# LoRA up projection in split precision instead of float32 in an attention plus mixture-of-LoRA kernel

## The reference

```
x = x + layernorm(attention(layernorm(x), wq, wk, wv, wo))       # 32 heads of 16, 8 kv heads, rotary, causal
n = layernorm(x)
h = n @ A^T            (8 experts x rank 16 = 128 columns)
logits = n @ W_gate^T  (8 experts), the two largest get softmax weights, the others 0
hw = h * (weight of its expert)
x = x + layernorm(n @ W_base^T + b_base + hw @ B)                # hw @ B: 128 -> 512, the LoRA up product
```

## Time and profile before

| | us |
|---|---|
| three runs | 270.4, 269.82, 265.75 |
| median of the runs | 269.82 |
| span of the profiled execution, first to last instruction | 265.6 |
| busy in it: PE, DVE, ACT, POOL | 212.1, 170.5, 135.9, 117.9 |

### The profile page before, as it was taken

How to read it: one execution, slowest core, us unless ns; L and a number is a source line. 1 busy time by engine, 2 the same in 40 slices (tenths; PEclk the granted TensorE clock), 3 DMA queues, 4 the chain that set the end, 5 groups by cost and what they waited for, 6 DMA issues and landing times.

```text
span 265.6 us, 3792 instructions
## 1 busy us (share of the span) xinstructions
PE 212.1 (80%) x1304; PEld 130.1 (49%) x1304; DVE 170.5 (64%) x414; ACT 135.9 (51%) x238; POOL 117.9 (44%) x93
## 2 busy tenths in 40 slices
PE   0699999977757999699595999695497988997860
PEld 0575734433433444244343444143477967886750
DVE  1983437759738768547473771426457988889674
ACT  2241603312235878558545574643157485777771
POOL 8000506613095867748466334941551452332031
PEclk9999999999979999979998899999979999998985
DMA  6994069898930638666473222223321001110013
GB/s 185 367 379 158 12 233 210 260 299 160 263 114 4 151 115 285 147 161 109 151 147 128 72 88 84 88 76 132 135 68 39 2 0 41 39 42 4 36 41 118
DMA packets 34058, 34.14 MB, mean 129 GB/s; under 512 B 2808, under 2 KB 28536, under 8 KB 34040
## 3 DMA queue, kind: packets, MB, share of 16 engines
q1 hardware_dynamic: 34040, 33.91, 43.8%
HBM read 19.42 MB, written 14.29 MB: 127 GB/s over the span
## 4 chain that ended last, share of the span: by engine, by line
PE 30%; DMA 28%; DVE 22%; ACT 7%; issue 5%; SPq 5%; POOL 2%; POOLq 0%; DVEq 0%; ACTq 0%
DMA region_b<-mrow 10%; DMA den_pk<-o_scr 6%; PE ps L1086 4%; PE ps L1149 4%; DVE stats L743 4%; PE ps L1001 3%; DMA o_scr<-o_sb 3%; PE ps L1060 3%; PE ps L1101 3%; PE ps L977 3%; PE ps L991 3%; DMA region_b<-q_scr 2%; SPq L325 2%; DMA rden_bc<-r_scr 2%; DMA x_sb<-x 2%
## 5 line engine op out<-in xcount | busy, mean ns | idle before, releaser
L917 DVE TENSOR_REDUCE nmax<-ps 128x4 f32<-128x1024 f32 x32 | 39.1, 1223 | 25.3 <-PE ps L1060 25.3
L512 POOL TENSOR_SCALAR_AFFINE_SELECT region_a<-region_a 128x1024 f32<-128x1024 f32 x32 | 35.2, 1106 | 26.7 <-ACT region_a L689 26.6
L1086 PE MATMUL ps<-region_b,kst 99*128 99x512 bf16 x96 | 28.7, 405 | 14.5 <-DMA region_b<-mrow 13.4
L689 ACT ACTIVATE region_a<-ps 128x1024 f32<-128x1024 f32 x32 | 32.7, 1020 | 1.2 <-PE ps L1086 1.2
L686 ACT ACTIVATE region_a<-ps 128x512 f32<-128x512 f32 x32 | 19.1, 598 | 26.0 <-PE ps L1086 25.6
L991 PE MATMUL ps<-region_a,region_c 128*128 128x512 f32 x64 | 29.0, 598 | 0.0
L914 DVE TENSOR_REDUCE nmax<-ps 128x4 f32<-128x512 f32 x32 | 21.8, 683 | 8.4 <-PE ps L1044 8.4
L554 ACT ACTIVATE std<-mv,eps_sb 128x1 f32<-128x1 f32 x32 | 9.3, 293 | 32.3 <-DVE mv L744 32.3
L1101 PE MATMUL ps<-region_a,v_aug 128*32 128x512 f32 x192 | 25.2, 603 | 0.0
L548 ACT ACT_TABLE_LOAD x17 | 21.8, 1283 | 1.1 <-PEq L1246 0.8
L1060 PEld LDWEIGHTS ps<-kst,region_b 96*128 96x128 bf16 x256 | 18.3, 102 | 7.0 <-issue 1.7
(11 more groups left out here) (107 smaller groups left out, 436.6 us busy)
## 6 DMA issues: line engine op xcount, KB each, us to landing
region_b<-q_scr SPq DMA_DIRECT2D x8, 768.0 KB, 8.0
o_scr<-o_sb SPq DMA_DIRECT2D x8, 512.0 KB, 3.1
q_scr<-region_c SPq DMA_DIRECT2D x8, 384.0 KB, 3.6
x_sb<-x SPq DMA_DIRECT2D x8, 256.0 KB, 5.9
q_scr<-region_c SPq DMA_DIRECT2D x8, 256.0 KB, 3.5
attn_t<-o_scr SPq DMA_DIRECT2D x8, 256.0 KB
rden_bc<-r_scr SPq DMA_DIRECT2D x8, 256.0 KB
out<-region_b SPq DMA_DIRECT2D x8, 256.0 KB, 2.0
```

The costliest lines, as they stand in the source:

```text
L512: pool.affine_select(out=blocks, in_=blocks, compare_op=ALU.is_ge, fill=0.0, base=0, pattern=[[0, 2], [0, REP], [1, P]], channel_multiplie ...
L689: nc.scalar.activation(probs[:, u % PRING, 1:3, :], ps[:, 4:6, :], ACT.Exp, scale=float(HEAD_DIM) ** -0.5).then_inc(exp_done, 1)
L917: nc.vector.tensor_reduce(nmax[:, gi % 2, 1, heads], ps[:, 1:3, :].rearrange("p a (r k) -> p r a k", r=REP), AX.XY, ALU.max, negate=True). ...
L1086: last = nc.tensor.matmul(ps[:, 3 + j, :], kst[0:TROWS, slot, k, kt * P:(kt + 1) * P], qst[0:TROWS, slot, k * REP:(k + 1) * REP, qt * P:(q ...
```

## The change

The up product becomes three float32r products, hw_h x B_h, hw_h x B_l and hw_l x B_h. The weights B get their high part on ACT and their low part on POOL in attention step 23. For the activations, ACT's copy of the transposed `hw` writes the rounded `hw_h`, and a new DVE instruction, `low_of_hw`, subtracts it from the same PSUM bank to give `hw_l`. It stands in DVE's step behind `ln_scale(1, s)` and ahead of `ln_scale(2, t1)`. PE waits for `hwt_low` instead of `hwt_ready`.

```diff
--- before.py
+++ after.py
@@ -64,7 +64,7 @@
 MATMULS_4 = (1, 1, 1, 1, 1)
 ROTATE_4, SPLIT_HIGH_4, SPLIT_MIDDLE_4, WRITE_4 = 5, 10, 12, 14
 
-SPLIT_WEIGHTS = {15 + j: j for j in range(8)}
+SPLIT_WEIGHTS = {15 + j: j for j in range(9)}
 CAT = DIM + EXPERTS * RANK + EXPERTS
 CATH = CAT // 2
 YB = DIM - CATH
@@ -105,6 +105,8 @@
         wo_l = over("wo_l", [P, REP, DIM], "wo_sb", 0)
         wcat_l = over("wcat_l", [P, KC, CAT], "wcat_sb", 0)
         lora_b_sb = sb("lora_b_sb", [P, DIM])
+        lora_h = sb("lora_h", [P, DIM], F32R)
+        lora_l = over("lora_l", [P, DIM], "lora_b_sb", 0)
         bias_sb = sb("bias_sb", [P, DIM])
         ident_sb = sb("ident_sb", [P, P])
         ident_bf = sb("ident_bf", [P, P], BF16)
@@ -154,7 +156,8 @@
         z1 = region_b[:, 0:1024].rearrange("p (a n) -> p a n", a=2)
         xn1_sb = region_b[:, 1024:2048].rearrange("p (a n) -> p a n", a=2)
         hw = region_b[:, 2048:2304].rearrange("p (a n) -> p a n", a=2)
-        hw_t = region_b[:, 2304:2560].rearrange("p (a n) -> p a n", a=2)
+        hw_h = over("hw_h", [P, 2, P], "region_b", 2304)
+        hw_l = over("hw_l", [P, 2, P], "region_b", 7680)
         xn1_h = over("xn1_h", [P, 2, KC, P], "region_b", 2560)
         xn1_l = over("xn1_l", [P, 2, KC, P], "region_b", 6656)
         y_sb = region_b[:, 3584:4608].rearrange("p (a n) -> p a n", a=2)
@@ -241,7 +244,8 @@
         gexp_ready = sem("gexp_ready")
         hw_ready = sem("hw_ready")
         hwt_psum = sem("hwt_psum")
-        hwt_ready = sem("hwt_ready")
+        hwt_high = sem("hwt_high")
+        hwt_low = sem("hwt_low")
         y_psum = sem("y_psum")
         y_ready = sem("y_ready")
         z2_ready = sem("z2_ready")
@@ -258,7 +262,7 @@
 
 
         quarters = [(w[:, j, :], h[:, j, :], l[:, j, :]) for w, h, l in ((wo_sb, wo_h, wo_l), (wcat_sb, wcat_h, wcat_l))
-                    for j in range(4)]
+                    for j in range(4)] + [(lora_b_sb[:, :], lora_h[:, :], lora_l[:, :])]
 
         def wait_o(engine, count):
 
@@ -661,7 +665,7 @@
                     act.wait_ge(hwt_psum, t3 + 1)
                     if t3 >= 2:
                         act.wait_ge(y_psum, t3 - 1)
-                    nc.scalar.copy(hw_t[:, t3 % 2, :], ps[:, 3, 0:P]).then_inc(hwt_ready, 1)
+                    nc.scalar.copy(hw_h[:, t3 % 2, :], ps[:, 3, 0:P]).then_inc(hwt_high, 1)
                 if 0 <= t4 < TILES:
                     sqrt(3, t4)
                 if 0 <= t2 < TILES:
@@ -850,6 +854,14 @@
                                         ga[:, 40:48].unsqueeze(2).broadcast_to([P, EXPERTS, RANK]), ALU.mult)\
                     .then_inc(hw_ready, 1)
 
+            def low_of_hw(t):
+
+                dve.wait_ge(hwt_high, t + 1)
+                if t >= 2:
+                    dve.wait_ge(y_psum, t - 1)
+                nc.vector.tensor_tensor(hw_l[:, t % 2, :], ps[:, 3, 0:P], hw_h[:, t % 2, :].bitcast(F32), ALU.subtract)\
+                    .then_inc(hwt_low, 1)
+
             def add_bias(t):
 
                 xb = 4 + 2 * (t % 2)
@@ -885,6 +897,8 @@
                                             xn1_h[:, t2 % 2, :, :].bitcast(F32), ALU.subtract).then_inc(xn1_low, 1)
                 if s < TILES:
                     ln_scale(1, s)
+                if 0 <= t3 < TILES:
+                    low_of_hw(t3)
                 if 0 <= t1 < TILES:
                     ln_scale(2, t1)
                     if t1 >= 2:
@@ -1155,15 +1169,20 @@
             def turn_hw(t):
                 pe.wait_ge(hw_ready, t + 1)
                 if t >= 1:
-                    pe.wait_ge(hwt_ready, t)
+                    pe.wait_ge(hwt_low, t)
                 nc.tensor.transpose(ps[:, 3, 0:P], hw[:, t % 2, :], ident_sb[:, :]).then_inc(hwt_psum, 1)
 
             def up_projection(t):
-                pe.wait_ge(hwt_ready, t + 1)
-                nc.tensor.matmul(ps[:, 4 + 2 * (t % 2), 0:CATH], hw_t[:, t % 2, :], lora_b_sb[:, 0:CATH],
-                                 start=False, stop=True, skip_group_check=True)
-                nc.tensor.matmul(ps[:, 5 + 2 * (t % 2), 0:YB], hw_t[:, t % 2, :], lora_b_sb[:, CATH:DIM],
-                                 start=False, stop=True, skip_group_check=True).then_inc(y_psum, 1)
+                if t == 0:
+                    pe.wait_ge(weight_low, 9)
+                pe.wait_ge(hwt_low, t + 1)
+                terms = ((hw_h, lora_h), (hw_h, lora_l), (hw_l, lora_h))
+                for i, (part, w) in enumerate(terms):
+                    nc.tensor.matmul(ps[:, 4 + 2 * (t % 2), 0:CATH], part[:, t % 2, :], w[:, 0:CATH],
+                                     start=False, stop=(i == 2), skip_group_check=True)
+                    last = nc.tensor.matmul(ps[:, 5 + 2 * (t % 2), 0:YB], part[:, t % 2, :], w[:, CATH:DIM],
+                                            start=False, stop=(i == 2), skip_group_check=True)
+                last.then_inc(y_psum, 1)
 
             def tile_step(s):
                 t2, t3 = s - 2, s - 3
```

## The result

Six runs of the changed kernel have a median of 278.76 us (276.7 to 279.81), six of the kernel before 270.11 (265.75 to 270.77). The ratio is 1.0391, with a 95% interval of 1.031 to 1.0472: slower, as forecast, with 280.1 us predicted and 274.0 to 283.0 as the range. Medians here are of all runs of a kernel, while a ratio and its interval compare only its fast runs with the fast ones of the kernel before, so a ratio is not the quotient of the medians beside it. The profiled execution took 279.17 us at a span of 277.4, so there are 1.8 us around the span (1.8 to 2.2 in the six runs).

What follows compares the result with a forecast made beforehand. DVE's instruction stream was taken as the bound. 2.40 (steps 3 and 4's first half) + 4 x 1.93 (steps 4 to 7) + 0 + 0.14 = 10.26 on the 269.82 us median gave 280.1 us, range 274.0 to 283.0.

Steps and rivals of the forecast that it cites:

- What bounds the kernel: In steps 5 to 7 of the last stage, DVE's instruction stream sets the step length; PE is just filled to it.
- The up product on PE: One tile's up product takes 0.75 us instead of 0.86, with 0.10 for the 188 wide float32r matmul.
- (d): Rival: the 188 wide float32r matmul runs at the float32 rate, adding 1.4 us in step 10: 281.5 us; chance 0.09.
- The wait: low_of_hw on DVE waits for ACT's copy behind z1 in steps 3 to 7: 1.31 us later, 1.10 of it waiting.
- The collision: Delayed line 750 on DVE is held under POOL's x + z1 until that ends: 0.62 us a step.
- (b): Rival: only the wait counts and line 750 isn't held, 5.4 us in all: 275.2 us; chance 0.10.
- Steps 3 and 4: Step 3 into step 4: delayed line 829 is held by POOL's division, net 2.40 us; both steps sum to 4.33.
- (a): Rival: line 829 of step 4 gets in ahead of POOL's division, 2.40 becomes 0.40: +8.3, 278.1 us; chance 0.20.
- The term of 2.40: Step 3 into step 4, net: DVE 2.74 us later behind held line 829, while 839, held 0.34 before, is free.
- Steps 8 to 10: About 0 in step 8, some 0.24 us in step 9, 0.33 less 0.43 in step 10: together 0.14 us.
- (c): Rival: PE is the bound, not DVE, so the wait fits into hidden slack: -0.9, 268.9 us; chance 0.06.
- (e): Rival: idle PE is granted the lower clock, some 0.7 us in each of 4 steps: +3, 283 us; chance 0.10.

## Why the prediction was right, and where its steps were not

**What bounds the kernel.** Right. DVE's stream set steps 6 and 7: the edits that moved or freed its waiting rows changed the step by the amount expected, and taking 0.11 us from PE in each tile changed nothing (7.86 us without low_of_hw). Only the removed line gave less than its 0.19 us, namely 0.06. PE was closer to being a second bound than I could tell, some 0.1 to 0.2 us a step.

**The up product on PE.** 0.75 us forecast, 0.75 measured; 0.09 us for the 188 wide matmul against the 0.10 I took. (d) falls.

**The wait.** Right in place, cause and size: 1.10 forecast, 1.00 of idle in the records and a step of 1.29 without the collision (9.15 - 7.86) against 1.31.

**The collision.** Right for line 750 in this kernel: forecast end 0.02 us behind POOL's row, measured 0.01, and 0.64 us of a step against 0.62. The rule as I drew it from the rows was too narrow. "Two tensors in SBUF" suggested that another form of line 750 would save the 0.62; it saved 0.09, since ln_apply was held in its place. (b) falls by the changed kernel's steps, with the kernel that adds later showing what (b) would have looked like.

**Steps 3 and 4.** The sum of 4.33 came out at 4.19, but by another road, and that is luck twice over. First, I left PE's clock at 1.00 in step 3. In the windows view of the changed kernel it was not:

```profile
202.95:208.30 5.35, 5.35 (x26) 5.31 (x27) 3.65 (x11) 2.85 (x6) 2.07 (x2) 0.68 0.15 44
```

PE had been idle for 3.57 us ahead of this (2.22 in the kernel before), came back at the lower of its two levels, 1.2 GHz, for part of the stretch, and so the copy that opens step 4 waited 0.73 us for it: step 3 took 9.74 us instead of the 8.83 forecast. In turn line 829 of step 4 (833 now) arrived 1.4 us into POOL's division instead of 0.27, and was held for 0.97 us, not 1.99. The errors are +0.91 in step 3 and -1.05 in step 4. PE's longer idle was there ahead of the changed part, and both edits of the kernel before show 3.57 us too, so it belongs to the execution rather than to the change. Second, (a) and my price for it assumed that the collision of step 4 is brought by the change. It isn't: it stands in kernels without the delay. Steps 3 and 4 take 20.48, 20.57 and 20.23 us in the three kernels with the wait (the changed one, with one input, with the later add), against 18.42 to 18.65 in the four without delay: some 1.9 us for the two steps, not 4.2. The term of 2.40 was read from the lucky profile, and against the other profiles it is some 2 us too large. This goes the way of the measured difference of medians, 8.65 us, being smaller than 10.3. That it is the whole of that gap isn't shown: the medians have a spread of several us, and the ratio of 1.0391 stands for some 10.5 us.

**Steps 8 to 10.** +0.14 forecast, -0.06 measured. In step 8 the new instruction waits 0.27 us and nothing is held, in step 9 0.17 us; the rest is within the idle times. The clock entered on both sides alike: in step 8 it was granted at 0.80 in the profile of the kernel before and at 0.79 in that of the changed one, while the kernel with the split alone and the one with the early copy had 1.00 there and took 7.30 us. Had only one of the two profiles had it, the difference would be off by about 1 us.

**The base.** I put the difference on the median of the runs because I knew of no time around the span. It is 1.8 us, so the profiled execution of before was one of about 267.4 us, a quick one. Measured from it the changed kernel's profiled 279.17 is 11.8 more, 9.91 from the last stage and 1.89 from the attention stage's spread.

(c) decided nothing: DVE had no hidden 1.1 us. Of the signs named, "steps 5 to 7 are 9.8 us apart" fits steps 6 and 7; step 5, 10.50 us before, is 12.43. "829 of step 4 is about 2.1 us long" doesn't fit: it is 1.13 (833 now), as told above. (e) came true only as far as it could do no harm: in step 5 PE was idle for 2.24 us, its next eight matmuls took 1.90 us instead of 1.46, and the step was still 1.93 us over that of the kernel before.

## What to carry to other kernels

An instruction put into a full in-order stream costs its wait, and the wait is set by what stands ahead of its input on the other engine: look there first, since moving one ACT copy by one place was worth 1.7 of 1.93 us a step. Then look at what the shifted instructions come to lie beside; a POOL tensor_tensor held small DVE instructions with two tensors in SBUF, a cast and tensor_scalars of 8 and 512 columns, and four short ones were better than one long one. One profile is one execution: a collision that hangs on a DMA's arrival should be looked for in several before it is booked on either side, since here it put some 2 us into a forecast of 10.

## What the runs showed of the hardware that I had not expected

A tensor_scalar of 128x512 (0.93 us instead of 0.54), one of 128x8 (0.78 instead of 0.29) and a cast of 128x2 (2.38 instead of 0.17) were held by a running POOL tensor_tensor as instructions with two SBUF tensors were, while reciprocals, batch norm statistics and a tensor_scalar of 128x1 (0.21) ran beside it. The Trainium skill, VectorE: DVE Perf Modes, Mode 2×_2P, has a mode for single-source instructions from SBUF to SBUF that reads through both ports; it asks that the outermost dimension of more than one element be even, or equal in source and destination. The one element instruction has no such dimension and went free, and those of 2, 8 and 512 didn't, which agrees with it; no run here shows an odd count above one. Removing a 128x1 DVE instruction that stood between two others gave 0.06 us, a third of its pitch, because the wait for the one ahead of it remained.
